# Inverse transform of a Fourier layer: all 64 rows at once, the column product in 64x64 tiles, GELU over two banks

## The reference, cut to what matters

```python
x = coords @ fc0_w + fc0_b                      # 3 -> 32 channels
for sw, cw, cb in layers:                       # four layers
    x1 = irfft2(modes(rfft2(x)) * sw)           # only 20 x 20 modes are kept and mixed over channels
    x2 = einsum('bchw,oc->bohw', x, cw) + cb    # 1x1 convolution
    x = gelu(x1 + x2)
x = gelu(x @ fc1_w + fc1_b)
h = (x @ fc2_w + fc2_b)[..., 0]
```

## Time and profile before

| | |
|---|---|
| median of 3 runs | 1637.08 us (1636.37 to 1639.5) |
| span of the profiled execution | 1633.9 us, 3.2 us below that median; no time of its own is given for that execution |
| TensorE busy | 1550.8 us, 95% |
| VectorE busy | 1190.1 us, 73% |
| ScalarE busy | 603.2 us, 37% |
| layers 0 to 2, one pair | 9.5 us |
| layer 3, one pair | 5.9 us |
| DMA | 316.30 MB, mean 194 GB/s |

### The profile page before, as it was taken

How to read it: one execution, slowest core, us unless ns; L and a number is a source line. 1 busy time by engine, 2 the same in 40 slices (tenths; PEclk the granted TensorE clock), 3 DMA queues, 4 the chain that set the end, 5 groups by cost and what they waited for, 6 DMA issues and landing times. The chain is left out here.

```text
span 1633.9 us, 44034 instructions
## 1 busy us (share of the span) xinstructions
PE 1550.8 (95%) x19928; PEld 896.7 (55%) x19928; DVE 1190.1 (73%) x1433; ACT 603.2 (37%) x929; POOL 92.3 (6%) x45
## 2 busy tenths in 40 slices
PE   9899999998999999999999999899999999989996
PEld 3555555555555555565555555777772115963332
DVE  3598899886989989878998998655540115887886
ACT  2433232223332232232322322444449996330221
POOL 1000000000000000000000000000000000007551
PEclk9999999999999999999999999999999999899998
DMA  6333332235655566556556556499998782037430
GB/s 218 114 125 130 128 133 104 120 125 214 247 231 233 207 225 237 215 177 256 214 214 237 222 209 231 139 362 356 354 354 330 255 287 72 1 73 186 110 85 13
DMA packets 59962, 316.30 MB, mean 194 GB/s; under 512 B 16576, under 2 KB 18688, under 8 KB 25984
## 3 DMA queue, kind: packets, MB, share of 16 engines
q1 hardware_dynamic: 36512, 177.99, 32.5%
q10 hardware_dynamic: 23264, 135.49, 20.2%
HBM read 176.09 MB, written 137.36 MB: 192 GB/s over the span
## 5 line engine op out<-in xcount | busy, mean ns | idle before, releaser
L835 ACT ACTIVATE act_c<-slots,conv_b 128x512 f32<-128x512 f32 x512 | 352.6, 689 | 734.0 <-PE slots L550 734.0
L550 PEld LDWEIGHTS slots<-inv_w,inv_out 128*128 128x128 f32 x4096 | 499.4, 196 | 188.2 <-issue 178.9
L550 PE MATMUL slots<-inv_w,inv_out 128*128 128x128 f32 x4096 | 541.8, 287 | 4.8 <-DVE inv_out L725 4.8
L725 DVE STREAM_TRANSPOSE inv_out<-slots 128x1024 f32<-128x1024 f32 x256 | 303.9, 1225 | 98.1 <-PE slots L515 98.1
L701 DVE STREAM_TRANSPOSE turned_h<-slots 128x1024 f32<-128x1024 f32 x200 | 237.9, 1228 | 27.5 <-PE slots L448 26.5
L690 DVE STREAM_TRANSPOSE turned_w<-act_c 128x1024 f32<-128x1024 f32 x192 | 224.9, 1208 | 1.1 <-ACT act_c L835 1.1
L448 PE MATMUL slots<-turned_w,fwd_w 32*64 32x512 f32 x3200 | 200.0, 607 | 3.0 <-DVE turned_h L701 2.5
L707 DVE STREAM_TRANSPOSE modes<-slots 128x640 f32<-128x640 f32 x96 | 81.0, 846 | 79.8 <-PE slots L460 79.8
L460 PE MATMUL slots<-turned_h,fwd_h 64*64 64x320 f32 x1600 | 136.4, 453 | 1.3 <-DVE turned_h L701 1.3
L537 PE MATMUL slots<-act_c,conv_w 32*32 32x512 f32 x3072 | 111.8, 604 | 19.3 <-DVE modes L707 15.4
L515 PE MATMUL slots<-turned_k,inv_h 32*64 32x320 f32 x2048 | 102.3, 455 | 8.3 <-DVE turned_k L715 6.9
(11 more groups left out here) (166 smaller groups left out, 1124.3 us busy)
## 6 DMA issues: line engine op xcount, KB each, us to landing
act_scratch<-act_c ACTq DMA_DIRECT2D x128, 1024.0 KB, 4.8
act_c<-act_scratch SPq DMA_DIRECT2D x128, 1024.0 KB, 5.2
mode_w<-in_sw_dram SPq DMA_DIRECT2D x20, 640.0 KB, 4.4
at_turned<-level_scratch SPq DMA_DIRECT2D x24, 256.0 KB, 4.2
at_ret_t<-level_scratch SPq DMA_DIRECT2D x20, 256.0 KB, 4.4
xin<-in_x_dram SPq DMA_DIRECT2D x4, 1024.0 KB, 8.1
turned_w<-in_x_turned_dram SPq DMA_DIRECT2D x3, 1024.0 KB, 5.9
at_straight<-level_scratch SPq DMA_DIRECT2D x10, 256.0 KB, 4.2
```

The costliest lines, as they stand in the source:

```text
L550: mm = nc.tensor.matmul(banks[:, p, at:at + 128], inv_out[:, t % 2, i, p, :, :, r].rearrange("p b o -> p (b o)"), inv_w[:, i, :], start=Fa ...
L725: nc.vector.transpose(dst, src).then_inc(inv_turned, 1)
L835: nc.scalar.activation(act_c[:, t % RING, :, p, :], banks[:, p, :].rearrange("p (i m) -> p i m", i=2), ACT.Gelu, bias=conv_b[:, l:l + 1]). ...
```

## The change

The inverse row transform takes 64 rows (even and odd row modes together) per matmul and gives all 64 image rows: in place of the second index "even or odd" of the output there is the index s of the half of the image. The table `inv_h` doubles to 128 columns, `inv_w` loses its signs and shrinks to 64 columns. `inverse_h` still has 8 matmuls, now of 64x64. `inverse_w` works on two banks at a time in 16 matmuls of 64x64 with 64 moving columns, where two banks had 8 matmuls of 128x128 with 128 columns. The GELU takes two banks in one instruction, and the semaphores `summed` and `act_set` count two per pair where they counted four. `keep_busy` uses the other table. The layout of `inv_out` gets the index s; the transposes into it have the same shapes.

```diff
-        inv_h = sb("inv_h", [128, 2, 64])
-        inv_w = sb("inv_w", [128, 2, 128])
+        inv_h = sb("inv_h", [128, 2, 128])
+        inv_w = sb("inv_w", [128, WW])
...
-        inv_out = sb("inv_out", [128, 2, 2, 4, 4, CH, 2])
+        inv_out = sb("inv_out", [128, 2, 2, 2, 2, 4, CH, 2])
...
-        def after_out(l, t, p):
-            return (l * PAIRS + t) * 4 + p + 1
+        def after_out(l, t, two):
+            return (l * PAIRS + t) * 2 + two + 1
...
                 for i in range(2):
-                    for kwh in range(2):
-                        for khh in range(2):
-                            b, half = 2 * kwh + khh, khh ^ i
-                            mm = nc.tensor.matmul(banks[half * 64:(half + 1) * 64, 4 + 2 * i + kwh, 0:320],
-                                                  inv_h[b * 32:(b + 1) * 32, l % 2, :],
-                                                  turned_k[b * 32:(b + 1) * 32, t % 2, i * 320:(i + 1) * 320],
+                    for s in range(2):
+                        for kwh in range(2):
+                            rows = slice(kwh * 64, (kwh + 1) * 64)
+                            mm = nc.tensor.matmul(banks[s * 64:(s + 1) * 64, 4 + 2 * i + kwh, 0:320],
+                                                  inv_h[rows, l % 2, s * 64:(s + 1) * 64],
+                                                  turned_k[rows, t % 2, i * 320:(i + 1) * 320],
                                                   start=True, stop=True)
                 mm.then_inc(inv_h_done, 1)
...
-            def inverse_w(l, t, p):
+            def inverse_w(l, t, two):
 
                 for i in range(2):
                     for r in range(2):
-                        at = i * 256 + r * 128
-                        mm = nc.tensor.matmul(
-                            banks[:, p, at:at + 128],
-                            inv_out[:, t % 2, i, p, :, :, r].rearrange("p b o -> p (b o)"),
-                            inv_w[:, i, :], start=False, stop=True, skip_group_check=True)
+                        for s in range(2):
+                            for half in range(2):
+                                for odd in range(2):
+                                    rows, at = slice(odd * 64, (odd + 1) * 64), i * 256 + r * 128 + s * 64
+                                    mm = nc.tensor.matmul(
+                                        banks[half * 64:(half + 1) * 64, 2 * two + odd, at:at + 64],
+                                        inv_out[rows, t % 2, i, two, s, 2 * half:2 * half + 2, :, r].rearrange(
+                                            "p b o -> p (b o)"),
+                                        inv_w[rows, :], start=False, stop=True, skip_group_check=True)
                 mm.then_inc(summed, 1)
...
                     conv(l, j)
-                    for p in range(2):
-                        inverse_w(l, j, p)
+                    inverse_w(l, j, 0)
                     if j >= 2 and not last:
                         pe.wait_ge(act_turned, after_turn(l + 1, j - 2))
                         if j + 1 < PAIRS:
                             pe.wait_ge(inv_turned, after_inv_turned(l, j + 1, 1))
                         dft_w(forward(l + 1, j - 2))
-                    for p in range(2, 4):
-                        inverse_w(l, j, p)
+                    inverse_w(l, j, 1)
                     if j >= 3 and not last:
-                        pe.wait_ge(act_set, after_out(l, j, 1))
+                        pe.wait_ge(act_set, after_out(l, j, 0))
                         dft_h(forward(l + 1, j - 3), (l + 1) % 2)
...
-                    for p in range(4):
-                        act.wait_ge(summed, after_out(l, t, p))
-                        nc.scalar.activation(act_c[:, t % RING, :, p, :],
-                                             banks[:, p, :].rearrange("p (i m) -> p i m", i=2), ACT.Gelu,
+                    for two in range(2):
+                        at = slice(2 * two, 2 * two + 2)
+                        act.wait_ge(summed, after_out(l, t, two))
+                        nc.scalar.activation(act_c[:, t % RING, :, at, :].rearrange("p i q m -> p q i m"),
+                                             banks[:, at, :].rearrange("p q (i m) -> p q i m", i=2), ACT.Gelu,
                                              bias=conv_b[:, l:l + 1]).then_inc(act_set, 1)
```

More of the change, by code:

```diff
@@ L63, in dft_constants @@
     fwd_h = np.zeros((2, 2, 2, 32, 2, 2, 32))
-    inv_h = np.zeros((2, 2, 2, 32, 2, 32))
+    inv_h = np.zeros((2, 2, 2, 32, 2, 2, 32))
     for parity in range(2):
@@ L76, in dft_constants @@
                     fwd_h[parity, :, 1, n, ph, kh % 2, at + 1] = cos[h, kh]
[L77 to L86, removed]
+        for p in range(4):
+            for n in range(32):
+                half, s, q, r = n // 16, n // 8 % 2, n // 2 % 4, n % 2
+                if p // 2 != half:
+                    continue
+                a, b = (p, q) if parity == 0 else (q, p)
+                h = 32 * s + 8 * a + 2 * b + r
+                for kh in range(MODES):
+                    at = kh // 2 * 2
+                    inv_h[parity, :, kh % 2, at, p % 2, 0, n] = cos[h, kh]
+                    inv_h[parity, :, kh % 2, at, p % 2, 1, n] = sin[h, kh]
+                    inv_h[parity, :, kh % 2, at + 1, p % 2, 0, n] = -sin[h, kh]
+                    inv_h[parity, :, kh % 2, at + 1, p % 2, 1, n] = cos[h, kh]
     kw = np.arange(MODES)
@@ L90, in dft_constants @@
     places = 16 * (kwh ^ place % 2) + place
[L91 to L97, removed]
+    inv_w = np.zeros((2, 2, 32, WW))
+    inv_w[:, 0, places] = norm * cos.T
+    inv_w[:, 1, places] = -norm * sin.T
     f32 = np.float32
@@ L101, in dft_constants @@
             inv_h.reshape(2, 128, -1).transpose(1, 0, 2).reshape(128, -1).astype(f32),
-            inv_w.reshape(2, 128, -1).transpose(1, 0, 2).reshape(128, -1).astype(f32))
+            inv_w.reshape(128, -1).astype(f32))
 def lift_mask():
@@ L307, in tower @@
         lift_consts = [(mask[:, :], k_lift_mask), (fc0_rows[:, :], fc0)]
-        rest = [(flat(inv_h[:]), k_inv_h), (flat(inv_w[:]), k_inv_w)]
+        rest = [(flat(inv_h[:]), k_inv_h), (inv_w[:, :], k_inv_w)]
         rest += [(conv_b[p * CH:(p + 1) * CH], cb) for p in range(4)]
@@ L409, in _ @@
                     if l == 0 and t % LIFT_E == LIFT_E - 1:
-                        sp.wait_ge(summed, after_out(0, t, 3))
+                        sp.wait_ge(summed, after_out(0, t, 1))
                     if l == 0 and t % LIFT_E == LIFT_E - 1 and t // LIFT_E + 2 < QUARTERS:
@@ L542, in keep_busy @@
                 for _ in range(n):
-                    nc.tensor.matmul(banks[:, b, 384:512], inv_w[:, 0, :], inv_w[:, 0, :], start=True, stop=True)
-            def inverse_w(l, t, p):
+                    nc.tensor.matmul(banks[:, b, 384:512], inv_h[:, 0, :], inv_h[:, 0, :], start=True, stop=True)
+            def inverse_w(l, t, two):
                 for i in range(2):
                     for r in range(2):
-                        at = i * 256 + r * 128
-                        mm = nc.tensor.matmul(
-                            banks[:, p, at:at + 128],
-                            inv_out[:, t % 2, i, p, :, :, r].rearrange("p b o -> p (b o)"),
-                            inv_w[:, i, :], start=False, stop=True, skip_group_check=True)
+                        for s in range(2):
[7 more added lines that the diff above has]
+                                        inv_w[rows, :], start=False, stop=True, skip_group_check=True)
                 mm.then_inc(summed, 1)
@@ L592, in _ @@
                 inverse_h(l, 1)
-                for p in range(1, 4):
-                    inverse_w(l, 0, p)
+                inverse_w(l, 0, 1)
                 for j in range(1, PAIRS):
@@ L663, in _ @@
             for _ in range(4):
-                nc.tensor.matmul(banks[:, 0, 0:128], inv_w[:, 0, :], inv_w[:, 0, :], start=True, stop=True)
+                nc.tensor.matmul(banks[:, 0, 0:128], inv_h[:, 0, :], inv_h[:, 0, :], start=True, stop=True)
         def mix_part(u, side, images=slice(0, IMAGES)):
@@ L720, in turn_inverse @@
                 if t >= 2:
-                    dve.wait_ge(summed, after_out(l, t - 2, 3))
+                    dve.wait_ge(summed, after_out(l, t - 2, 1))
                 for i in range(2):
                     src = flat(banks[:, 4 + 2 * i:6 + 2 * i, :]).rearrange("p (n o k) -> p o n k", o=CH, k=2)
-                    dst = inv_out[:, t % 2, i].rearrange("p a b o r -> p o (a b) r")
+                    dst = inv_out[:, t % 2, i].rearrange("p a s b o r -> p o (a s b) r")
                     nc.vector.transpose(dst, src).then_inc(inv_turned, 1)
```

12 lines of the change are left out of this document (6 added, 6 removed).

## The result

The change makes the kernel slower: 1688.88 us (1679.65 to 1697.41, 4 runs) against 1636.72 us before in the same comparison, ratio 1.0308 [1.0255, 1.0361]. The forecast was 1602 us, range 1580 to 1618. The profiled execution took 1695.4 us, its span 1693.6.

A forecast was written before the change was run, and what follows sets the result against it. The prediction took a TensorE loop of 9.49 us as the bound in layers 0 to 2, and DMA to limit layer 3. Gains of 24 + 12 - 1 = 35 us from 1637 gave 1602 us, range 1580 to 1618.

The forecast's parts named there:

- the column product (iw): TensorE's column product: 32 instructions at 30.5 ns, 0.98 us a half (bounds 0.6 to 2.56), saving 2.2 us a pair.
- inverse_h: Inverse row transform on TensorE: 1.36 us, with L725 starting 1.42 us after it, 0.52 us later than before.
- Rival B: Inverse row transform costs more than dft_h: total 1635 us at 1.80 us, 1618 at 1.6; chance 0.10.
- E: TensorE stays as it was in effect, quadrants not overlapping enough: total 1637 us; chance 0.04.
- Layers 0 to 2: Bank loop becomes the longest, period 9.24 us after 9.49; gain 8.1 us a layer, 24 us for three.
- Layer 3: Last layer's period: 4.65 us by engines alone, 5.64 us by DMA, from 5.95; gain 12 us.
- the DMA wall: In layer 3, transfers of 2.097 MB a pair at 370 to 374 GB/s hold the period at 5.64 us.
- Rival A: The DMA limit in layer 3 gives way, period 4.65 us: total 1575 us, or 1585 at 5.0; chance 0.17.
- GELU: ScalarE's GELU over two banks takes 1.11 us; conv's last one is 0.42 us longer, covered in layers 0 to 2.
- Clock: TensorE's granted clock: 1 us charged in all for longer idle gaps at layer starts; stays 1.00 inside a layer.
- rival D: Clock falls in the steady loop; in a third of the periods, 31 us lost, time about 1633 us; chance 0.04.
- Rival C: Column product's small matmuls cost 80 ns each, 2.56 us a half: about 1770 us; decisive from 61 ns; chance 0.05.

The follow-up runs named there:

- a2: Changed kernel with half of the column product left out (no second image of each pair); 1591.92 us, one run.
- c1_wide_second: Changed kernel with the second half of the column product (banks 2 and 3) as 64x128 tiles; 1659.43 us, ratio 1.0136.
- d2: Kernel before with the new scheme in layers 0 to 2, three quarters of the column product in layers 1 and 2 as 64x128 tiles; 1615.13 us, ratio 0.9895.
- c2_wide_both: Changed kernel with both halves of the column product as 64x128 tiles, still 64 moving columns; 1666.8 us, ratio 1.0192.
- d1: Kernel before with the new scheme in layer 0 only; 1622.17 us, ratio 0.9913.
- a1: Changed kernel with the store and load of the activations cut to 128 of 2048 columns; 1586.99 us, one run.
- b1: Kernel before with only the GELU changed, to two banks at a time; 1654.06 us, ratio 1.0113.
- a4: Changed kernel with the store and load of the activations cut to 1024 of 2048 columns; 1605.42 us, one run.

## Why the prediction was wrong, step by step

**The step that failed is the column product (iw)**, and in two ways. It was priced as TensorE time only: so many instructions by so many ns. That they have to be brought by DMA, 16 KB per 256, stood in no term. And they were counted wrong: the loops over i, r, s, half and odd give 32 matmuls for two banks, 64 issued instructions and 64 weight loads, where the prediction and the description of the change have 16 and 32 (before, two banks took 16 and 16). With the right count the price per instruction was too high, 18.6 ns and not 30.5, and the two errors nearly cancelled: a half takes 1.19 us, forecast 0.98, within its bounds. Neither made any difference to the period.

What the count means for a block shows in one table (us that the loop leaves for 256 instructions, at the period without stops):

```
before, layers 0 to 2     9.48 x 256/256 = 9.5    no stops
before, layer 3           5.94 x 256/160 = 9.5    no stops
after, layers 0 to 2      9.05 x 256/448 = 5.2    some stops
after, layer 3            4.62 x 256/352 = 3.4    stops all through
a2, layer 3               4.62 x 256/224 = 5.3    stops
c1_wide_second, layer 3   5.56 x 256/288 = 4.9    stops
c1, layers 1 and 2        9.05 x 256/384 = 6.0    some stops
d2, layers 1 and 2        9.12 x 256/352 = 6.6    almost none
c2_wide_both, layer 3     6.33 x 256/224 = 7.2    none
```

The limit could have been read before the change. The page shows the queue, and the mixing product, the one stage with many small matmuls in a row, stopped in the same way (the kernel before; the earlier trace rows is the same stage of another layer, and I read only the length of its matmuls):

```profile
q8 instruction: 158, 2.59, 0.6%
```

```profile
373.68 4.33 PE L501 MATMUL slots<-modes,mode_w 64*64 64x128 f32 x139 [0.33 <-DVE modes L707]
379.40 8.05 PE L501 MATMUL slots<-modes,mode_w 64*64 64x128 f32 x253 [1.39 <-issue]
```

The 1.39 us end at number 193 modulo 256, 1.41 us after a packet. A share of 0.6% of 16 engines says nothing against a bound: no two packets of this queue overlap in any of the traces, and one takes 0.95 us.

The Trainium skill, Runtime: NRT & Kernel Launch (Instruction fetch mechanics), describes the refill in 16 KiB blocks of 256 instructions by a DMA queue of the sequencer; the packets here agree. It calls the cost of crossing into a new block mostly hidden. So it is in the kernel before, at 9.5 us a block; at 3.4 us it is not, and the measurement decides.

**inverse_h**: right. 1.31 us, with L725 1.37 us after its start, forecast 1.36 and 1.42. Rival B falls, and so does E, by the 1.19 us of a half.

**Layers 0 to 2**: the loop was right and a little better than forecast: 7.62 + 0.06 + 1.37 = 9.05 us, forecast 9.24. Where fetching doesn't disturb, a layer gains more than the 8.1 us forecast: layer 0 gained 11.7, in d1 13.4. In layers 1 and 2 stops of up to 2.6 us gave it back. Those layers also load while they store (226 GB/s in the window of layer 1 above); layer 0 does little but store (126 GB/s from 110 to 340 us), which fits its few stops.

**Layer 3**: 4.62 us without stops, forecast 4.65 by engines alone; then the step was wrong in naming the DMA wall as what comes next. The instruction fetch came first, at a mean of 7.50. Of the 89 us between 31 periods at 4.62 and the 232.3 measured, 27 remain with thin transfers (a1: 170.7 us), and 62 come with the traffic. Rival A, that the DMA wall gives way, was not put to the test by the change; in a2 the transfers reached 371 GB/s, as in the earlier trace rows, and no more.

**GELU**: 1.11 us was right, and that it costs nothing in the new loop too; b1 shows what it costs without the shorter product.

**Clock** (step and rival D): forecast 1 us, the clock never leaving 1.00 inside a layer. In layer 3 it was 0.86, part of the time at 1.2 GHz, after the stops: L514 takes 2.36 us there, not 1.31. It follows the stops: in a1, with stops of 1.7 us at most, it is 0.99, and in a4, with stops of up to 2.9 us, 0.96. In the steady loop of layers 0 and 1 it kept 1.00 and 0.99 (110 to 340 and 400 to 667 us), so D, which had it fall there, did not come. The price in layer 3 is open. TensorE was busy 170.1 us there and 145.0 us in a1 with the same instructions, so of the 62 us that come with the traffic up to 25 are slower execution and 37 are idle time. How much of the 25 would have become longer stops at the full clock, no run separates.

**Rival C** had the side and the words, "small matmuls cost by the piece", and the wrong place. TensorE executes them at 18.6 ns. C's threshold of 61 ns was for 32 instructions a half; for 64 it is 31 ns, still well above. The piece is paid for in the program's bytes. A chance of 0.08 for slower rested on a price for the engine only, and no rival had a supply of instructions that runs short.

## What to carry to other kernels

Multiply every change of tile shape out to issued instructions, matmuls and weight loads both, and divide the period by the blocks of 256 that it needs: in this kernel 6.6 us a block ran nearly undisturbed beside 1 MB transfers, 5 to 6 us had stops where loads ran beside the stores, and 3.4 us stopped throughout. Look for idle time put down to "issue" in the middle of a group of matmuls, and at the packets of the instruction queue, before trusting the busy time. The change pays where the loop is held by another engine and has time per block (layer 0 here, 0.9% by itself), not in a short loop beside heavy transfers.

## What the runs showed that was not expected

- Only one block of 256 instructions was read ahead of TensorE in the stopping stretches, and from its landing to its first instruction 1.2 to 1.5 us passed. Even with 26 GB/s of other traffic a block took about 4 us (legs of 1.48, 0.98 and 1.43 us).
- With the same instructions, traffic lengthens only the time until the fetch starts (1.48, 1.92, 2.94 us at 26, 162 and 263 GB/s), not the fetch of 0.95 us. What the fetch stands behind there is not shown by these records, nor why it was 2.14 us at 327 GB/s in the kernel before.
- An instruction of 64x64 with 64 columns takes 18.6 ns, one of 64x128 with the same columns 66 ns.
- Cutting the 1 MB transfers in four cost 40 us, most of it in layers 1 and 2; the cause is open.
